# Last expert layer: thirteen of sixteen token tiles dispatched to slots from inside the cross attention, three computed densely

## The reference

```
# second cross attention, 16 heads of 8, 1500 keys
attn = softmax(rope(x @ Wq.T) @ rope(ctx @ Wk.T).T * 8 ** -0.5)
x = x + (attn @ (ctx @ Wv.T)) @ Wo.T
# last expert layer, on xn = layernorm(x): one shared and 8 routed experts, hidden width 256
shared = (silu(xn @ Gs) * (xn @ Us)) @ Ds
probs  = sigmoid(xn @ router.T + bias)              # 8 experts
scores, indices = top_k(probs, 2); scores /= sum(scores)
w      = scores put at indices, 0 elsewhere
routed = sum over e of w[:, e] * ((silu(xn @ G[e]) * (xn @ U[e])) @ D[e])
x = x + shared + routed
```

## Time and profile before

| | us |
|---|---|
| median of 3 runs (lowest, highest) | 1519.72 (1514.0, 1524.32) |
| the profiled execution, device time | 1509.65 |
| its span, first to last instruction | 1507.9 |
| PE / PEld busy | 1352.3 / 923.6 |
| DVE / ACT / POOL busy | 1105.7 / 820.5 / 784.4 |
| chain that ended last: PE, ACT, DVE | 42%, 10%, 5% of the span |

### The profile page before, as it was taken

One profiled execution on the slowest core, in us unless ns is written; L12 is line 12 of the kernel. 1 busy time (PEld: TensorE's weight loads), 2 busy tenths in 40 slices (PEclk: granted clock), 3 DMA queues, 4 the chain that ended last, 5 costly groups with the idle time before them and its releaser, 6 DMA issues.

```text
span 1507.9 us, 41832 instructions
## 1 busy us (share of the span) xinstructions
PE 1352.3 (90%) x17179; PEld 923.6 (61%) x17179; DVE 1105.7 (73%) x1832; ACT 820.5 (54%) x1804; POOL 784.4 (52%) x736
## 2 busy tenths in 40 slices
PE   6888999999979985769999999999999999789998
PEld 4557888788946662436656665666666566555554
DVE  6885767757768878648888888888888888335554
ACT  3442344356623431537777777777777777723332
POOL 6675322424676666727777777777777772000000
PEclk9878999999989998879999999999999999989999
DMA  4004400026214034464644464454455454204230
GB/s 129 2 2 130 159 2 2 18 79 192 62 30 72 22 51 94 96 122 122 133 120 130 116 135 123 124 125 127 123 129 130 120 130 105 65 11 104 62 62 13
DMA packets 77088, 134.71 MB, mean 89 GB/s; under 512 B 18081, under 2 KB 56867, under 8 KB 73635
## 3 DMA queue, kind: packets, MB, share of 16 engines
q1 hardware_dynamic: 74850, 127.84, 34.4%
q0 software_dynamic: 2048, 4.20, 0.9%
HBM read 100.54 MB, written 34.73 MB: 90 GB/s over the span
## 4 chain that ended last, share of the span: by engine, by line
PE 42%; ACT 10%; DVE 5%; issue 3%; POOL 1%; DMA 1%; SPq 0%; ACTq 0%; POOLq 0%; DVEq 0%
PE ps L2186 11%; PE ps L916 7%; PE ps L2170 7%; ACT ARENA L2341 4%; PE ps L928 4%; PE ps L2133 3%; PE ps L2124 3%; PE ps L2147 2%; DVE ARENA L2261 2%; ACT ARENA L2319 2%; ACT ARENA L2325 2%; ACT ARENA L2332 1%; PE ps L2195 1%; PE ps L2155 1%; DVE ARENA L2271 1%
## 5 line engine op out<-in xcount | busy, mean ns | idle before, releaser
L2261 DVE TENSOR_REDUCE ARENA<-ps 112x2 f32<-112x1000 f32 x384 | 456.7, 1197 | 116.0 <-PE ps L2147 109.2
L2341 ACT ACTIVATE ARENA<-ps 125x448 f32<-125x448 f32 x768 | 378.3, 549 | 136.6 <-PE ps L2170 135.7
L2391 POOL TENSOR_TENSOR ARENA<-ARENA 64x500 f32<-64x500 f32 x192 | 227.8, 1187 | 109.2 <-ACT ARENA L2319 90.3
L2170 PEld LDWEIGHTS ps<-ARENA 64*125 64x125 bf16 x3072 | 122.6, 134 | 134.4 <-ACT ARENA L2341 71.6
L2170 PE MATMUL ps<-ARENA 64*125 64x112 bf16 x3072 | 169.4, 229 | 20.5 <-ACT ARENA L2341 19.3
L2186 PE MATMUL ps<-ARENA 125*17 125x112 f32 x6144 | 185.6, 262 | 0.0
L127 POOL TENSOR_TENSOR rs<-rs,mhalf 128x1 f32<-128x1 f32 x96 | 73.3, 765 | 178.9 <-DVE rs L122 178.6
L2147 PE MATMUL ps<-ARENA 64*112 64x500 bf16 x768 | 152.7, 387 | 10.0 <-DVE ARENA L2261 9.7
L2186 PEld LDWEIGHTS ps<-ARENA 125*17 125x17 f32 x6144 | 136.8, 98 | 32.2 <-issue 21.9
L2402 POOL TENSOR_TENSOR ARENA<-ARENA 128x500 bf16<-128x500 f32 x96 | 129.3, 1348 | 44.7 <-ACT ARENA L2325 44.7
L2397 POOL TENSOR_TENSOR ARENA<-ARENA 128x500 f32<-128x500 f32 x96 | 122.1, 1272 | 18.0 <-DVE ARENA L2254 11.8
(11 more groups left out here) (273 smaller groups left out, 2394.9 us busy)
## 6 DMA issues: line engine op xcount, KB each, us to landing
ARENA<-key_parts SPq DMA_DIRECT2D x192, 187.5 KB, 3.7
ARENA<-in_ctxT SPq DMA_DIRECT2D x96, 250.0 KB, 3.6
key_parts<-ARENA SPq DMA_DIRECT2D x64, 375.0 KB, 2.6
ARENA<-token_weights SPq DMA_DIRECT2D x16, 512.0 KB, 5.2
slots<-in_c_blank SPq DMA_DIRECT2D x2, 1472.0 KB, 12.5
results<-ARENA SPq DMA_DIRECT2D x42, 64.0 KB, 3.2
ARENA<-in_L_ffn_W SPq DMA_DIRECT2D x1, 2048.0 KB, 8.6
ARENA<-in_L_ffn_W SPq DMA_DIRECT2D x4, 512.0 KB, 10.3
```

The lines of the kernel that those rows point to most:

```text
L2170: m = e.matmul(ps[0:KT, b1[h], 112 * g:112 * g + 112], KS[b % 4][r, g, KT * kt:KT * kt + KT], Q1[r, b % 2, 112 * g:112 * g + 112], start=T ...
L2261: e.tensor_reduce(mxp[0:112, b % 2, 2 * g:2 * g + 2, ch], ps[0:112, b1:b1 + 2, 0:500], AX, ALU.max) \
L2341: e.activation(Pb[0:KT, n % NP_, 448 * h:448 * h + 448], ps[0:KT, b1[h], 0:448], ACT.Exp, bias=0.0, scale=1.0).then_inc(exped.sem, 1)
L2391: e.tensor_tensor(T2[r:r + 64, :], T0[64 - r:128 - r, n % 2, :], sin[64 - r:128 - r, sl], ALU.mult) \
```

## The change

- **Stage 5 has slots.** Tiles 0 to 12 (`LAST_SPLIT = 13`) are dispatched: their routed experts are computed in 30 slots (`LAST_SLOTS`). A slot on PE is four matmuls of 128 columns (`up`) and two (`down`); on ACT one `Silu` of 256 columns and a copy of 128; on DVE one product of 256 columns and a weight copy of 768 columns.
- **Dense remainder.** After the slots come 12 "wide" steps: four for the shared expert on 448 columns each, and one per routed expert on the 336 columns of tiles 13 to 15. Their down product has the tokens as weights, two matmuls of 128 columns per tile, so it comes out as rows and is added straight to `XR` (`wide_add`).
- **Work placed in stage 4.** Constants and the blanking of the DRAM slots are loaded at its start. Routing of tiles 0 to 11 at batch 26, key tile 3; of tile 12 at batch 27, key tile 11; exponential, count and the parts of `choose` at batch 28, key tiles 0 to 11; 26 scatters, one per key tile from batch 28, key tile 10, to batch 30, key tile 11; the expert weights at batch 29; the slots' load at batch 31, key tile 1, weight copies at 4 to 8, the first two groups of transposes at 9 and 10. `begin` (the first two `up`) stands ahead of the last two `apply`.
- **Layer norm of a tile** is no longer one tile late: `norm` at key tile 3, `scale` at 8, `finish` at 9 of the same batch. The last tile's steps are spread over slots 2 to 10, and stage 5 waits for no `end` of stage 4.
- The DVE choice for tiles 13 to 15 runs in ten parts beside the slots and the first wide steps. Gathers start when the last eight slot results have landed.

```
+LAST_SPLIT = 13
+LAST_SLOTS = (2 * 112 * LAST_SPLIT + 8 * 127) // 128
...
-                    for kt, step in ((1, "out"), (3, "norm"), (7, "finish")):
+                    for kt, step in ((1, "out"), (3, "norm"), (8, "scale"), (9, "finish")):
...
+                if b == B - 12:
+                    f[3].append(("cast", 0))
+                if b == B - 6:
+                    f[3].append(("route", 0))
+                if b == B - 5:
+                    f[11].append(("route", 1))
+                if b == B - 4:
+                    f[0].append(("exp", 0))
+                    for i, part in enumerate(("chances", "first", "others", "second", "picks")):
+                        f[1 + i].append(("choose", part))
+                    f[6].append(("count", 0))
+                    for i, part in enumerate(("counts", "bases", "places", "table", "shares")):
+                        f[7 + i].append(("choose", part))
+                for n in range(2 * LAST_SPLIT):
+                    at_b, kt = divmod(NK * (B - 4) + 10 + n, NK)
+                    if b == at_b:
+                        f[kt].append(("scatter", n, NK * b + kt))
+                if b == B - 3:
+                    f[6].append(("weights", 0))
+                if b == B - 2:
+                    f[6].append(("clear_pads", 0))
+                if b == B - 1:
+                    f[1].append(("slots_in", 0))
+                    for i in range(5):
+                        f[4 + i].append(("copy_weights", i))
+                    f[9].append(("turn_slots", 0))
+                    f[10].append(("turn_slots", 1))
...
+                    if n == B * NK:
+                        yield ("begin", 0)
...
+            def up(e, w, i):
+                g, k = divmod(i, 4)
+                bk = up_bank(i)
+                w.wait_ge(*x_cp(g + 1))
+                w.wait_ge(*w_cp(i + 1))
+                w.wait_ge(*free[bk])
+                for c in range(4):
+                    m = e.matmul(ps[:, bk, 128 * c:128 * c + 128], WT[:, i % NW, 128 * c:128 * c + 128],
+                                 XST[:, g % 3, 128 * k:128 * k + 128], start=True, stop=True)
...
+            def pe(e, w):
+                for i in range(2, N1 + 2):
+                    if i < N1:
+                        up(e, w, i)
+                    tail(e, w, "pe", i)
+                    if i == 13:
+                        route(e, w, 2, 0)
+                    down(e, w, i - 2)
+                    for g in range(2, len(groups)):
+                        if 4 * g - 3 == i:
+                            turn_slots(e, w, g)
+                w.wait_ge(*weights_in(len(loads)))
+                for q in range(NJ + 1):
+                    if q < NJ:
+                        wide_up(e, w, q)
+                    if q:
+                        wide_out(e, w, q - 1)
...
+            def copy_weights(e, w, i):
+                w.wait_ge(*weights_in(len(loads)))
+                w.wait_ge(*sel(32))
+                if i >= NW:
+                    w.wait_ge(*down_mm(i - NW + 1))
...
+                e.tensor_copy(WT[:, i % NW, :], recs[:, bass.ds(v * REC, REC)]).then_inc(w_cp.sem, 1)
...
+            def dve(e, w):
+                for i in range(N1):
+                    tail(e, w, "dve", i)
+                    multiply(e, w, i)
+                    if i >= 2 and i + 3 < N1:
+                        copy_weights(e, w, i + 3)
+                    if i == 14:
+                        choose_late(e, w, 0)
+                for q in range(NJ + 1):
+                    if q < NJ:
+                        wide_multiply(e, w, q)
+                    if q:
+                        wide_add(e, w, q - 1)
+                    if 1 <= q < 4:
+                        for part in range(3 * q - 2, 3 * q + 1):
+                            choose_late(e, w, part)
+                    for t in combine_after.get(q, ()):
+                        combine(e, w, t)
...
+            def gather(e, w, t):
+                for i in range(N1 - 8, N1):
+                    w.wait_ge(*landed(i))
+                w.wait_ge(*ln(TURN, 5, NT - 1))
+                w.wait_ge(*scattered(2 * T))
+                if t >= 8:
+                    w.wait_ge(*combined(t - 8))
...
+            def scatter(e, w, n):
+                t, k = divmod(n, 2)
+                w.wait_ge(*blank_in(2))
+                w.wait_ge(*ln(NX, 5, t))
+                w.wait_ge(*sel(28))
```

More of the change, by code:

```diff
@@ L2002, in l1_xattn @@
             at, ring, pair = {}, 0, 0
-            for step in order():
+            for step in [*order(), ("fold", B - 1), ("turn", B - 1), ("out", NT - 1), ("finish", NT - 1)]:
                 if step[0] == "peak":
@@ L2009, in l1_xattn @@
                     ring += 2
-                elif step[0] in ("keys", "values", "full", "fold", "turn", "out", "finish"):
+                elif step[0] in ("keys", "values", "full", "fold", "turn", "out", "finish", "route", "count"):
                     at[step] = ring % 3
```

790 lines of the change are left out of this document (508 added, 282 removed).

## The result

The changed kernel took 1442.62 us (median of 4, 1439.86 to 1443.77) beside 1516.93 us for the kernel before in the same series: ratio 0.9515, 95% interval 0.9482 to 0.9548. The forecast was 1443. The profiled execution took 1441.94 us with a span of 1440.1, where 1433 and 1431 were forecast. So the agreement of the medians is partly luck: the profiled execution came 9 us later than my sum, and the 10 us that I added for the distance between profiled execution and median were not needed. The distance was 0.7 us this time.

What follows compares the result with a forecast made beforehand. The replaced stretch was taken as bound by PE, six-matmul steps of 4.51 us. Span 1507.9 - 188.1 + 101.4 + 10 = 1431 us, 1433 device time; with the 10 us median offset kept, 1443; range 1427 to 1466.

Steps and rivals of the forecast that it cites:

- From P to the end: P: two of the last four `apply` done; from there to the span's end 101.4 us, replacing 188.1.
- Slots: Thirty expert slots bound by PE's weight loads at 94% filled: 44.8 us, 1.5 per slot.
- the start: First two `up`, last two `apply`, table load, first `Silu` and bank copy before the third `up`: 3.2 us.
- The wide steps: Four shared and eight routed dense steps after the slots, PE-bound: 19.2 and 28.7, together 47.9 us.
- The two weighed rules: Gathers blocked by DVE combinations, end 3 us later; table-switch drain of 1.38 us, start 4.6 instead of 3.2.
- Ahead of P: Work added before two of the last four `apply` are done: 9.7 us, with the count's matmuls 10.
- The moved finish: Layer norm's `norm`, `scale`, `finish` moved: taken at nothing, covered by transposes of `full`; without cover 15 times 0.3, 4.5 us.
- Routing in batch 26: Routing of 12 tiles where PE has about 1 us free: 24 records, 2.7 us, all counted.
- The choice in batch 28: Expert choice on DVE: 9.3 us and about 1 in gaps, against 3.9 free; taken at 6, bounds 2.5 to 9.
- Batch 31: Eight transposes on PE and two copies on ACT: between 0 and 2, taken at 1.0 us.
- Rival 4: Clock stays at its lower level, 1.2 GHz, once DVE has starved PE in batch 28: 1563 us; chance 0.03.
- Blanking and issues, scatters: Blanking and 11 issues on SP: 0 to 4 us, taken at nothing; 26 scatters on nearly idle POOL, also nothing.

Runs made afterwards that it cites:

- e9_copy_twice: Changed kernel with each slot's weight copy on DVE followed by a second, unread one; 100.4 us from two of the last four `apply` done to the span's end.
- e4: Changed kernel with the routing of twelve tiles in batch 26 cut into four pieces at key tiles 1, 3, 5 and 7; 1446.43 us, ratio 0.9549.
- e1_finish7: Changed kernel with scale and finish put back to key tiles 6 and 7 instead of 8 and 9; 1437.7 us, ratio 0.9491.

## Why the prediction was right, and where it was not

**From P to the end**, 101.4 forecast, 100.4 measured in seven traces of the first chip within 0.1. Slots bound by weight loads, 34.00 of 34.00; the doubled weight copy shows that nothing else was near. I took 94% from the first expert layer and it was 100%: from the third `up` at 1343.3 to the first wide step at 1386.5 are 43.2 us, forecast 44.8; the start ahead of it took 3.5, forecast 3.2. The wide steps took 48.3 to the last addition at 1434.7 (47.9), the end 5.4 (5.5). The spread tail is worth 6.1 us, and the sum was right to price it at its records alone.

**The two weighed rules.** The gathers took 0.94 to 1.02 us beside the combinations and those 0.34 to 0.35: the contention that the Trainium skill (SBUF — State Buffer, Who interferes with whom) names did not show at this place. It showed where I had not applied it, at the moved scaling. The `Silu` began at 1341.35, right behind the table load (1340.06, 1.28 long). The drain that the Trainium skill (ScalarE: Activation LUTs, What ACT_TABLE_LOAD costs) adds did not show, and the start cost 3.5 and not 4.6, with 0.6 of it a wait for the copy of batch 31's result.

**Ahead of P**, 10 forecast, 19.9 measured:
- *The moved finish, taken at nothing*, is the step that failed. I had named the cover (the transposes of `full`) and the price without it (15 times 0.3). It costs 0.38 to 0.45 us in each odd batch: 5.3 in batches 2 to 25 and 0.4 in batch 27 are 5.7 us, more than my upper bound of 4.5. The scaling is 1.28 us long, not 0.35, where it stands beside POOL's blend.
- *Routing in batch 26*, 2.7 forecast: 4.0 and 4.8 in the two executions. The records took 2.8. The batch was 0.8 longer than with the routing in pieces, in part by the lower clock; at full clock (e9_copy_twice) it added 3.6.
- *The choice in batch 28*, 6 forecast, 5.4 and 6.4 measured in the two executions, with the clock at 0.93 and 0.80 in it. Right in size and in part by luck. I had taken DVE's total against its slack (10.3 less 3.9). DVE's busy time rose by 6.7 only, where the list of `choose` had given 9.3, and PE's longest wait was for one piece of the choice. Spread out, batches 28 and 29 together came to 43.0 instead of 45.1 (38.7 before), with the choice's instructions unchanged, so order and clock make up 2.1 of the 6.4 us; how the other 4.3 divide is open.
- *Batch 31*, 1.0 forecast: 0.6 at full clock (e4), 2.1 to 6.5 with the clock as it fell. Rival 4 in a small form: the lower level came, for 3 to 20 us instead of to the end.
- *Blanking and issues, scatters*: nothing, as taken. The copy of batch 1 stands within the spread of executions, and POOL's last scatter ended at 1320.9 with nothing waiting behind it.

- *Batches 27 and 29*, left at nothing: 0.8 and 1.0, of which 0.4 are the finish.

**What it adds up to.** Of the 9.9 us missed 5.7 are the finish, 1.3 the routing, 1.4 the rest of batches 27 and 29, 1.1 batch 31 and 1.4 the run's own; about 1 goes off for the choice and the count. The median came out at the forecast because 10 us of distance between median and profiled execution were in it, which the new series did not have. The lower end of the range does not come out of the terms named for it: 1443 less 3.5, 1, 2.5 and 5 is 1431, not 1427. The measurement lies inside either.

No version tried is faster than the changed kernel beyond the uncertainty: e1_finish7 is the nearest (0.9491 against 0.9515 and 0.9546, with 4.6 us of it seen batch by batch, and 2.4 of them lost again in batch 26 of its trace).

## What to carry to other kernels

An instruction that is moved without a change can become four times as long by what runs beside it on another engine (1.28 us instead of 0.34 here): look at POOL's timeline at the new place, not only at who waits for whom. Where one engine serves another in order, price extra work by the instruction that it is put in front of, not by the engine's idle total. And a gain won ahead of a stretch in which PE idles in part can be lost there to the clock, which is read only from several traces of the same kernel.
